# Moving the statistics of a layer norm from VectorE to ScalarE, with order changes around it, in a kernel of adapters, Mamba layers and experts

## The reference, cut to what matters

```python
# 1. language adapter, by sequence, with its own layer norm
h = relu(x @ W1[lang] + b1[lang]);  a = x + h @ W2[lang] + b2[lang]
a = (a - mean(a)) * rsqrt(var(a) + 1e-5) * gamma[lang] + beta[lang]
# 2. four Mamba layers on the residual stream a
for l in range(4):
    y = (a - mean(a)) * rsqrt(var(a) + 1e-5) * ln_w[l] + ln_b[l]     # the norm of the change
    xs, z = split(y @ W_in[l].T)                                    # 256 inner channels each
    u = silu(causal_conv4(xs) + conv_b[l])
    dt, B, C = split(u @ W_x[l].T);  dt = softplus(dt @ W_dt[l].T + b_dt[l])
    state = exp(dt * A) * state + dt * B * u       # 16 states per channel, scan over time
    a = a + ((sum_s(C * state) + u * Dp[l]) * silu(z)) @ W_out[l].T
# 3. a weighted sum of 8 SwiGLU experts and a shared one, for every token (dense)
# 4. a router takes the two best of 8 GELU experts for each token (sparse); their weighted sum is added
```

## Time and profile before

| | us |
|---|---|
| median of three runs | 2651.08 (2651.05 to 2653.18) |
| the profiled execution, its own time | 2652.19 |
| its span, first to last instruction | 2650.4 |
| busy: PE, DVE, POOL, ACT | 2367.8 (89%), 2057.3 (78%), 2047.8 (77%), 1563.2 (59%) |
| mean granted TensorE clock | 0.951 of full |

### The profile page before, as it was taken

How to read it: one execution, slowest core, us unless ns; L and a number is a source line. 1 busy time by engine, 2 the same in 40 slices (tenths; PEclk the granted TensorE clock), 3 DMA queues, 4 the chain that set the end, 5 groups by cost and what they waited for, 6 DMA issues and landing times. The chain is left out here.

```text
span 2650.4 us, 22739 instructions
## 1 busy us (share of the span) xinstructions
PE 2367.8 (89%) x6064; PEld 1052.7 (40%) x6064; DVE 2057.3 (78%) x2025; ACT 1563.2 (59%) x2433; POOL 2047.8 (77%) x1269
## 2 busy tenths in 40 slices
PE   6688988889888999999999999999998899999586
PEld 4233333333333333333343333333333344444364
DVE  4899999999999999988998999899989443333221
ACT  4676777777775667666666666666666233222132
POOL 4699999999997799988899888888889432321276
PEclk9799999999999999999999999999999999999798
DMA  7565455644556766666666666566666500100254
GB/s 232 191 212 204 157 181 203 215 170 142 173 184 215 245 230 232 232 222 215 222 235 222 214 224 226 207 219 226 224 231 205 179 21 9 36 10 9 65 113 64
DMA packets 216892, 464.88 MB, mean 175 GB/s; under 512 B 29436, under 2 KB 109122, under 8 KB 216770
## 3 DMA queue, kind: packets, MB, share of 16 engines
q1 hardware_dynamic: 204786, 455.30, 51.0%
q0 software_dynamic: 11264, 7.98, 1.9%
q10 hardware_dynamic: 720, 0.23, 0.0%
HBM read 440.00 MB, written 23.99 MB: 175 GB/s over the span
## 5 line engine op out<-in xcount | busy, mean ns | idle before, releaser
L893 DVE TENSOR_TENSOR_SCAN hh<-decays,psdB 128x1024 f32<-128x1024 f32 x512 | 1165.6, 2283 | 53.4 <-ACT decays L715 20.0
L1030 POOL TENSOR_TENSOR products<-hh,Clo 128x1024 f32<-128x1024 f32 x408 | 961.5, 2360 | 153.7 <-DVE hh L893 150.9
L454 PE MATMUL psY<-products,ident 128*128 128x512 f32 x1708 | 820.1, 604 | 90.2 <-POOL products L1030 54.9
L715 ACT ACTIVATE decays<-dt,Acur 128x508 f32<-128x508 f32 x1024 | 668.0, 708 | 5.9 <-DVE hh L893 5.5
L882 DVE TENSOR_TENSOR psdB<-psT,Blo 128x1024 f32<-128x1024 f32 x395 | 484.1, 1226 | 65.7 <-ACT psT L683 32.6
L454 PEld LDWEIGHTS psY<-products,ident 128*128 128x128 f32 x1708 | 320.3, 193 | 525.8 <-issue 369.4
L1458 DVE TENSOR_TENSOR ac<-sg,d_bank 128x512 f32<-128x512 f32 x135 | 92.8, 688 | 225.4 <-PE d_bank L1308 175.6
L434 PE MATMUL psW<-xnT,wcur 128*128 128x512 f32 x496 | 227.2, 600 | 34.9 <-ACT u L646 18.9
L1030 POOL TENSOR_TENSOR products<-hh,late 128x1024 f32<-128x1024 f32 x104 | 244.1, 2367 | 11.7 <-PE psY L454 11.7
L728 ACT ACTIVATE late<-psdB 128x512 f32<-128x512 f32 x153 | 90.6, 592 | 233.0 <-PE psT L502 177.8
L1034 POOL TENSOR_TENSOR products<-products 128x512 f32<-128x512 f32 x170 | 215.6, 1268 | 13.3
(11 more groups left out here) (215 smaller groups left out, 3035.2 us busy)
## 6 DMA issues: line engine op xcount, KB each, us to landing
Blo<-rows SPq DMA_DIRECT2D x280, 512.0 KB, 6.0
Clo<-rows SPq DMA_DIRECT2D x280, 512.0 KB, 5.2
late<-rows SPq DMA_DIRECT2D x104, 512.0 KB, 6.5
wcur<-taps_l SPq DMA_DIRECT2D x31, 512.0 KB
fw<-in_Wg SPq DMA_DIRECT2D x36, 256.0 KB, 5.6
fw<-in_Wu SPq DMA_DIRECT2D x36, 256.0 KB, 4.5
fw<-in_Wd SPq DMA_DIRECT2D x36, 256.0 KB, 5.1
disp<-fw SPq DMA_DIRECT2D x16, 528.0 KB, 7.8
```

Source lines behind the costliest of these rows:

```text
L454: ins = pe.matmul(psY[:, :], lhsT=ident[:, :], rhs=gg[k % NGB][:, j, :], start=False, stop=(k % NK == NK - 1 and j == last - 1))
L715: ins = act.activation(dA[k % NDA][:, j, :, 1:T], dt[i % 2][:, c, :, 1:T], ACT.Exp, scale=Acur[i % 2][:, s:s + 1])
L893: dve.tensor_tensor_scan(out=hh[k % NHB][:, :, :].rearrange("p c t -> p (c t)"), data0=dA[k % NDA][:, :, :, :].rearrange("p c q t -> p (c ...
L1030: ins = pool.tensor_tensor(gg[k % NGB][:, :, :], hh[k % NHB][:, :, :], tile(Clo, Chi, slot(i, s)), ALU.mult)
```

## The change

Seven edits go together.

1. For iterations from 2 on, the mean and the variance are made by ACT: `mean` (after `turn0` at step 2: four instructions of Identity with scale -1/128 and `accum_out`), `variance` (step 3: four of Square with bias -mean and `accum_out`) and `root` (step 5: one instruction, 128x4). DVE's `statistics` remains for iterations 0 and 1. POOL's `deviation` keeps the power and the product.
2. From iteration 15 on, `time_step` moves from POOL to DVE, behind the scan of step 11, and `time_input` from POOL's step 11 to step 12, behind `gate0`.
3. `PAIRED` gains steps 4 and 10: from iteration 15 on POOL adds two more pairs, PE does two matmuls less per iteration.
4. Before iteration 0: relu(6), copy_xT(7), relu(7) on ACT, hidden(6), condition(6) on PE and adapt(7) on DVE come earlier, first_dt, dt1 later.
5. Sparse phase: a half's transposes leave `up` and become `turn`. PE's order per expert is turn(e,1), up(e,0), up(e,1), turn(e+1,0), down(e,0), down(e,1); DVE's is turned(e,1), address(e), pick(e+1,0), turned(e+1,0), pick(e+1,1), weigh(e,0), weigh(e,1). The loops are unrolled.
6. Expert 0's slots load in two pieces, so that the first half can start earlier.
7. The very last half is weighed in four pieces, each followed by its own indirect DMA.

```diff
-ACT_AT = {1: ["params", "dtu1", "norm"], 2: ["turn0"], 4: ["sums1", "x0"], 5: ["x1"], 6: ["z0"], 7: ["z1", "silu"], ...
+ACT_AT = {1: ["params", "dtu1", "norm"], 2: ["turn0", "mean"], 3: ["variance"], 4: ["sums1", "x0"], 5: ["x1", "root"], 6: ["z0"], ...
-POOL_AT = {1: ["gate1"], 6: ["rstd"], 10: ["dt"], 11: ["dtu"], 12: ["gate0"]}
+POOL_AT = {1: ["gate1"], 6: ["rstd"], 10: ["dt"], 11: ["dtu"], 12: ["gate0", "dtu_late"]}
-PAIRED = [0, 2, 3, 5, 7, 8, 9, 13, 14, 15]
+PAIRED = [0, 2, 3, 4, 5, 7, 8, 9, 10, 13, 14, 15]
@@ ScalarE @@
+                def mean(t):
+                    if layer(t) > 0:
+                        act.wait_ge(wfree, W["out", t - ROUND] + 1)
+                    else:
+                        act.wait_ge(h_ok, group(t) + 1)
+                    act.wait_ge(wready, W["T", t - 1] + 1)
+                    act.wait_ge(rstd_ok, t)
+                    for q in range(G):
+                        ins = act.activation(xc[:, q, :], h_res[:, group(t) * G + q, :], ACT.Identity, scale=-1.0 / D, accum_out=negm[:, q:q + 1])
+                    ins.then_inc(moment_ok, 1)
+                def variance(t):
+                    act.wait_ge(moment_ok, 2 * (t - 2) + 1)
+                    for q in range(G):
+                        ins = act.activation(xc[:, q, :], h_res[:, group(t) * G + q, :], ACT.Square, bias=negm[:, q:q + 1], accum_out=vare[:, q:q + 1])
+                    ins.then_inc(moment_ok, 1)
+                def root(t):
+                    act.wait_ge(moment_ok, 2 * (t - 2) + 2)
+                    act.activation(vare[:, :], vare[:, :], ACT.Identity, scale=1.0 / D, bias=K["eps"][:, 0:1]).then_inc(root_ok, 1)
@@ VectorE @@
-                        if k == 6 and i + 2 < NIT:
-                            statistics(i + 2)
                         input_term(i, k)
...
                         scan_step(i, k)
+                        if k == 11 and FIRST <= i < NIT - 1:
+                            time_step(i + 1)
@@ GpSimd, deviation @@
+                    if t > 1:
+                        pool.wait_ge(root_ok, t - 1)
+                        pool.tensor_tensor(rstd[:, :], vare[:, :], K["nhalf"][:, :], ALU.pow).then_inc(rs2, 1)
+                        pool.wait_ge(rs2, t + 1)
+                        pool.tensor_tensor(nmr[:, :], negm[:, :], rstd[:, :], ALU.mult).then_inc(rstd_ok, 1)
+                        return
@@ sparse phase, TensorE @@
-                def body(e, p, j):
-                    up(e, p, j, 0)
-                    up(e, p, j, 1)
-                    down(e, p, 0)
-                    down(e, p, 1)
+                turn(0, 0)
+                for e in range(NE):
+                    turn(e, 1)
+                    up(e, 0)
+                    up(e, 1)
+                    if e + 1 < NE:
+                        turn(e + 1, 0)
+                    down(e, 0)
+                    down(e, 1)
```

More of the change, by code:

```diff
@@ L43 @@
 SUM_FIRST = (7, 15)
-ACT_AT = {1: ["params", "dtu1", "norm"], 2: ["turn0"], 4: ["sums1", "x0"], 5: ["x1"], 6: ["z0"], 7: ["z1", "silu"], 8: ["bcdt"], 10: ["turn1"], 11: ["dt0"],
+ACT_AT = {1: ["params", "dtu1", "norm"], 2: ["turn0", "mean"], 3: ["variance"], 4: ["sums1", "x0"], 5: ["x1", "root"], 6: ["z0"], 7: ["z1", "silu"], 8: ["bcdt"], 10: ["turn1"], 11: ["dt0"],
           12: ["sums0", "dt1", "softplus"], 13: ["outT"], 14: ["added"], 15: ["centre", "dtu0"]}
 GIVEN = {4: 0, 9: 5, 13: 8}
-POOL_AT = {1: ["gate1"], 6: ["rstd"], 10: ["dt"], 11: ["dtu"], 12: ["gate0"]}
+POOL_AT = {1: ["gate1"], 6: ["rstd"], 10: ["dt"], 11: ["dtu"], 12: ["gate0", "dtu_late"]}
 G_AT = [-11, -9, -7, -6, -5, -4, -2, 0, 1]
@@ L800, in _ @@
                                 centre(i + 2)
+                            if what == "mean" and i + 2 < NIT:
+                                mean(i + 2)
+                            if what == "variance" and i + 2 < NIT:
+                                variance(i + 2)
+                            if what == "root" and i + 2 < NIT:
+                                root(i + 2)
                             if what == "outT" and i > 0:
@@ L910, in statistics, with time_step @@
                     ins.then_inc(moments, 1)
+                def time_step(t):
+                    dve.wait_ge(ln_ok, t)
+                    whole = dt[t % 2][:, :, :, :].rearrange("p c q t -> p (c q t)")
+                    dve.tensor_tensor(whole, whole, soft[:, :, :].rearrange("p c t -> p (c t)"), ALU.add).then_inc(dt_ok, 1)
                 def act_product(n):
@@ L1498, in at_least, with last, sums @@
                 eng.wait_ge(sm, v)
-        def experts(eng, body):
-            with eng.Fori(0, NE // 2) as j:
-                body(2 * j, 0, j)
-                body(2 * j + 1, 1, j)
+        def last(h):
+            return h == NHT * NE - 1
+        def sums(h, q, n):
+            return psH[q][:, 0:128] if last(h) else psE[h % NHT][:, 128 * q:128 * (q + n)]
         with nc.Block() as block:
@@ L1573, in _ @@
                 act.sem_inc(gelud, CR)
-                def body(e, p, j):
-                    for c in range(NHT):
-                        h = NHT * e + c
-                        at_least(act, downed, CR + h - 1)
-                        for f in range(NF):
-                            act.wait_ge(upped, CR + NF * h + f + 1)
-                            act.activation(ht[c][:, f, :], psH[f][:, :], ACT.Gelu).then_inc(gelud, 1)
-                experts(act, body)
+                for h in range(NHT * NE):
+                    c = h % NHT
+                    at_least(act, downed, CR + h - 1)
+                    for f in range(NF):
+                        act.wait_ge(upped, CR + NF * h + f + 1)
+                        act.activation(ht[c][:, f, :], psH[f][:, :], ACT.Gelu).then_inc(gelud, 1)
             @block.vector
```

124 lines of the change are left out of this document (68 added, 56 removed).

## The result

The changed kernel takes 2667.93 us (median of 6 runs, 2661.33 to 2671.81) against 2651.26 for the kernel before (6 runs, 2651.05 to 2653.75): a ratio of 1.0065, with a 95% interval of 1.0051 to 1.0079. It is slower, by 0.65%. Executions of one kernel differ with the granted clock (27 of the kernel before on one chip: ten took 2643.6 to 2647.9 us at a mean clock of 0.953 to 0.958, seventeen took 2650.2 to 2655.9 at 0.950 to 0.952, and one more at 3101.4 and 0.756 is left out), so a median of several and the trace of a single one can stand some us apart. The profiled execution takes 2668.1 us with a span of 2666.38; that of before had 2652.19 and 2650.44.

The account below looks back on a forecast made before the run. Bound taken: a POOL-PE-ACT-DVE loop in iterations 1 to 12, PE's full stretch and DVE's scans in 16 to 29. Terms +7.7, -3.0, 0.0, -0.9, +0.2, +10 gave +14 on 2652.2, 2666; median forecast 2665, range 2632 to 2698.

Parts of the forecast that it names:

- First kind, +7.7: Iterations 1 to 12: ACT's mean and variance outlast its 4.26 us pause, x0's copy 0.6 us later each, +7.7 us.
- a sign of being wrong: The forecast would be wrong if x0's copy on ACT came no later than before.
- Rival A: Accumulator nearly free, 3.3 us for both sets: iterations 1 to 12 unchanged, 16 to 29 -12 us, total 2636; chance 0.27.
- Iterations 13 to 15, -3.0: DVE runs almost without waits there, so losing the statistics saves 1.0 us in each of three iterations.
- Iteration 30, -0.9: This iteration has no mean on ACT, so it was to be 0.9 us shorter.
- Start, 0: Earlier first scans gain nothing, since PE's x0 of iteration 1 waits for weights by DMA: 0 us.
- Third kind, 0.0 an iteration: Iterations 16 to 29: statistics -1.0, deviation -0.4, pairs -0.86 and variance's pause ahead of x1 +2.25 sum to 0.0 us.
- 1.0 each: Iterations 16 to 29, step 6 on DVE: without statistics the next product follows sooner, 1.0 us less per iteration.
- time_step to DVE, time_input one step later, 0 either way: Iterations 16 to 29: DVE's waits take up its added 1.23 us, POOL loses 2.36 and gains two adds of 1.27: 0.
- 0.86 less: Iterations 16 to 29: step 10's new pair takes 0.86 us off PE's full stretch; step 4's pair gives nothing.
- Clock, +10: New PE pauses were to bring 6 more low-clock stretches, each at most 1.7 us: +10 us, 0 to 32 possible.
- Sparse, +0.2: Sparse phase: the pick waits for slots, 17.5 us an expert, +1.2 for six; first expert about 1 sooner; +0.2.

Follow-up runs that it names:

- Experiment 3: The kernel before with only the new sparse phase added: 2660.4 us, ratio 1.0034 to the kernel before.
- experiment 1: The kernel before with only mean, variance and root moved to ACT (variance at step 3): 2647.1 us, ratio 0.9989 to the kernel before.
- experiment 2: The changed kernel with statistics back on DVE and the old deviation on POOL: 2655.0 us, ratio 1.0016 to the kernel before.
- experiment 5: The changed kernel with time_step and time_input back on POOL at their old steps: 2666.3 us, ratio 1.0054 to the kernel before.
- experiment 6: The changed kernel with the old list of ten paired steps: 2661.6 us, ratio 1.0037 to the kernel before.
- (10): The kernel of experiment 9 with the pairs of steps 4 and 10 added on POOL: 2645.0 us, ratio 0.9966 to the kernel before.
- Experiment 8: The changed kernel with the next expert's first transposes between the two halves of down: 2658.9 us, ratio 1.0026 to the kernel before.
- experiment 9: The kernel of experiment 1 with variance behind x0's copy and the sparse phase with transposes between down's halves: 2631.6 us, ratio 0.9913 to before.
- experiment 12: The changed kernel with variance behind x0's copy, transposes between down's halves, gate0 at step 15, time_input at 13: 2645.1 us, ratio 0.9967 to before.
- experiments 8 to 12: The five kernels with the next expert's first transposes between the halves of down: 2658.9, 2631.6, 2645.0, 2646.5 and 2645.1 us.

## Why the prediction was right or wrong

The forecast was 2665 and slower; 2667.93 was measured. The total is closer than the terms deserve: it is a sum of errors that cancel, so its closeness is luck.

- *First kind, +7.7: wrong, 0.* The failed step is the price of the accumulator. I took 4.9 us for both sets and called nothing below 3.3 possible, since eight instructions of centre's kind cost that; they cost 2.7. centre's 0.481 has two column operands (scale and bias), mean's has none and variance's one (0.295 and 0.389). The Trainium skill, ScalarE: Activation LUTs ("What ACT_TABLE_LOAD costs") adds about 93 ns for each column operand and gives 293 and 387 for 128 elements; the trace agrees within 2 ns. Reading the accumulator costs only the overlap with the next activation: the next starts 0.385 behind this one's start, not 0.29. With 2.7 the pause of 4.26 hides it all, and x0's copy comes no later there, which the prediction had named as a sign of being wrong. Rival A's place was right, its price still too high. The rule that the prediction quotes under rival A from the Trainium skill, ScalarE: Activation LUTs ("Rules for kernel authors"), by which the edit should lose time, isn't borne out by the runs: the norm's edit alone is at 0.9989 of before, and placed behind x0's copy at 0.9913.
- *Iterations 13 to 15, -3.0: measured -2.8, but not by the edit.* Experiment 3 shows the same without it, and experiment 1 no more with it: the hit is luck.
- *Iteration 30, -0.9:* the stretch from there to the last scan is 1.6 shorter.
- *Start, 0: right*, once the disturbance of +2.9 is taken off.
- *Third kind, 0.0 an iteration: +0.67.* The pause ahead of x1 is there, 1.12 where my lower price gave 1.4. With that price the sum was -0.85 an iteration (rival A), and it is +0.67. Two steps failed. The first is "1.0 each" for the statistics: VectorE arrives 1.0 earlier at the scan of step 7 and waits 1.0 there for ScalarE's decays, in all 14 iterations of all ten kernels with the norm's edit. That is what I had for the first kind. The second is "time_step to DVE, time_input one step later, 0 either way", with the pairs' "0.86 less". time_step doesn't disappear in VectorE's waits: its step takes 0.8 to 0.9 longer, and it draws POOL's product out by 1.0. The moved time_input and step 10's pair (1.27) stand in front of the product for which PE waits before x0. Without the norm's edit this order still gains 7.2 (experiment 2). Added to the norm's edit, the pairs cost 8.6 (experiment 5) and time_step 9.3 (experiment 6, in the trace 3.8 above its median); added where the pause is gone, the pairs cost 13 by the medians and 18 by the traces (10).
- *Clock, +10: the sign is wrong in the loop.* I counted more low stretches for more pauses. In iterations 16 to 29 there are 14 instead of 23, 58 us instead of 89; behind 2490 us, in the sparse phase, 5 instead of 1. So more pauses went with fewer low stretches in the loop; why is not shown.
- *Sparse, +0.2: +8.1.* The mechanism stands in the prediction, with the pick waiting for slots, and PE's pause was put at 2.3. It is 2.0 to 3.8, and the four of 3.5 and more are followed by a low clock: 20.3 for such an expert instead of 17.5. Experiment 8 takes both away with one move.

So the two true costs are +9.4 in the third kind and +8.1 in the sparse phase, where the forecast had 0.0 and 0.2 and put 7.7 and 10 in other places.

Where the 18.4 us lie can be read from VectorE's scans. The table has the mean time, in us, from the start of one step's scan to that of a later one, over iterations 16 to 29; the norm alone is experiment 1, the order alone experiment 2:

| from scan to scan, steps | before | norm alone | order alone | both (after) |
|---|---|---|---|---|
| 3 to 5 (VectorE waits for PE behind x1) | 9.55 | 10.80 | 9.51 | 10.89 |
| 5 to 7 (statistics, or a wait for decays) | 8.81 | 8.73 | 8.83 | 8.73 |
| 11 to 12 (time_step) | 4.52 | 4.48 | 5.45 | 5.34 |
| 13 to 14, and 15 to the next step 0 | 9.95 | 8.74 | 8.56 | 8.36 |
| all others | 35.58 | 35.54 | 35.55 | 35.76 |
| iteration | 68.42 | 68.29 | 67.90 | 69.08 |

The norm costs 1.2 in the first row, the order 0.9 in the third, and nearly all of both prices stays when the two meet. What pays for them is the same in both: waits of VectorE in the fourth row, 1.75 an iteration before, 0.46 with the norm, 0.34 with the order, 0.11 with both. Each edit alone takes that slack (-1.22 and -1.40), and together they can take it only once (-1.60). That is 1.02 of the 1.31 an iteration that the meeting costs. Of the 1.75, 0.51 are waits for a DMA, nearly all of this row of the kernel before (1050 to 1930 us):

```profile
DVE psdB L882 <- DMA Blo<-rows: 7.1, 4, 2.7
```

Experiment 3, with the same loop, has 6.2 of it in iterations 16 to 29; the kernels of experiments 1, 2 and 9 and the changed one have 0.7 at most. What stays open is why these late waits shrink with either edit, and what PE's wait for POOL has to do with the time. That wait is 29.9 to 40.3 between 1050 and 1930 us in all kernels that have the norm and the pairs or time_step, and 19.7 to 23.9 in those with the norm alone, the order alone or neither; but experiment 12 has the longest of them and a loop shorter than most of the others. Kernels with the pairs alone or time_step alone on the old statistics were not run.

## What to carry to other kernels

When three engines are each about 90% busy, two edits that gain alone can lose together, because both are paid by the same slack; try each alone before both (here -1.8 and -7.2, and +9.4 together), and look whether the slack that each used is still there. Put new work on an idle engine behind the copy that releases the bound engine, not ahead of it: one place in the list of steps was worth 12.9 us with the new order. Asking for the next item's data ahead of the current item's second half needs a buffer that is free by then; one half later it was free, and 8 us came back.

## What the runs showed of the hardware

- An accumulating activation of 128 x 128 is an ACTIVATE of 0.295 us (0.389 with a column bias) and a read of 0.19. Start to start that is 0.29 and 0.385.
- Fewer low stretches of the clock can pay for a pause: with the norm's edit PE was busy 14.2 us less for the same matmuls, idle 12.5 more. In experiment 9 they are the whole gain: busy 24.4 less, idle 0.5 less.
- POOL's product of 128 x 1024 takes 2.36 us. The one during which VectorE runs time_step took 3.25 to 3.36, in all 14 iterations of each of the eight kernels with that move; every other one in those 14 iterations took at most 2.40, in all fourteen kernels.
- From the end of POOL's last scatter issue to the next expert's first one it takes 2.4 to 2.8 us in the five kernels of experiments 8 to 12, but 3.7 to 6.0 where SP's loads of the next weights and slots were issued 0.5 to 6.4 us before that end.
- The same loop started 2.7 us later and took 3.0 less in iterations 13 to 15 in another execution: terms of that size need a second trace before they are given to an edit.
